# Graph layer on one Trainium2 core: target rows in 16 bits, and the sixteen first feature loads of the node pass issued in steps

## What is computed

```python
row, col = (edge_index[0], edge_index[1])          # src, dst
tp = fctp_messages(node_features[col], edge_attr_tensor, W1, W2, W3, W4)
messages = tp @ Wm + bm
agg = jax.ops.segment_sum(messages, row, num_segments=N_NODES)
upd = jnp.concatenate([node_features, agg], axis=-1) @ Wu + bu
return node_features + upd
...
x = _layernorm(x + ref(x, ...), axis=-1)
```

## Time and profile before

| | |
|---|---|
| median of 3 runs | 1828.5 us (1827.64 to 1835.35) |
| profiled execution, its own time | 1834.27 us |
| its span, first to last instruction | 1832.5 us |
| mean granted TensorE clock | 0.957 of full speed |
| busy: PE, DVE, ACT, POOL | 1581.1, 1594.1, 900.5, 1067.6 us |
| moved by the DMA engines | 490.07 MB, mean 267 GB/s |

### The profile page before, as it was taken

One profiled execution on the slowest core, in us unless ns is written; L12 is line 12 of the kernel. 1 busy time (PEld: TensorE's weight loads), 2 busy tenths in 40 slices (PEclk: granted clock), 3 DMA queues, 4 the chain that ended last, 5 costly groups with the idle time before them and its releaser, 6 DMA issues.

```text
span 1832.5 us, 35242 instructions
## 1 busy us (share of the span) xinstructions
PE 1581.1 (86%) x11572; PEld 876.3 (48%) x11572; DVE 1594.1 (87%) x1825; ACT 900.5 (49%) x1721; POOL 1067.6 (58%) x837
## 2 busy tenths in 40 slices
PE   4167899999999999999999999999999999298882
PEld 2033444545444554545544454445554454276662
DVE  6276699999999999999999999999999996199994
ACT  1123444545444444555544444445554445088885
POOL 3005777777767777776777777767777774211110
PEclk8688999999999999999999999999999999699996
DMA  9996678888888888888888888888888885899994
GB/s 378 404 395 178 157 234 248 245 244 244 256 244 247 246 247 255 256 247 244 249 255 248 243 250 256 248 242 246 246 252 249 255 248 139 287 391 421 416 418 170
DMA packets 174618, 490.07 MB, mean 267 GB/s; under 512 B 48664, under 2 KB 99096, under 8 KB 149484
## 3 DMA queue, kind: packets, MB, share of 16 engines
q1 hardware_dynamic: 91980, 379.42, 57.5%
q0 software_dynamic: 82304, 109.12, 27.2%
q10 hardware_dynamic: 288, 0.95, 0.2%
HBM read 393.10 MB, written 96.31 MB: 267 GB/s over the span
## 4 chain that ended last, share of the span: by engine, by line
DMA 33%; issue 21%; PE 18%; DVE 14%; POOL 9%; ACT 2%; SPq 1%; POOLq 1%; DVEq 0%; ACTq 0%
DMA agg<-summed,row_idx 18%; DVE prod L527 7%; POOL agg L344 6%; DMA agg<-start_rows 5%; DMA prod<-agg 5%; DMA e_sb<-in_e_rep 4%; PE ps L671 4%; PE ps L678 3%; POOL xg L326 3%; PE ps L659 2%; DVE prod L596 2%; DVE prod L515 2%; DVE stats L615 2%; PE ps L733 1%; PE ps L722 1%
## 5 line engine op out<-in xcount | busy, mean ns | idle before, releaser
L344 POOL DMA_INDIRECT agg<-summed,row_idx x392 | 625.4, 1595 | 363.7 <-DMA agg<-summed,row_idx 183.2
L527 DVE TENSOR_TENSOR prod<-ps,e_sb 128x2048 f32<-128x2048 f32 x294 | 655.3, 2285 | 68.3 <-DMA e_sb<-in_e_rep 47.5
L678 PE MATMUL ps<-prod,packed_sb 128*32 128x512 f32 x2744 | 672.4, 607 | 0.8 <-ACT S_sb L398 0.8
L326 POOL DMA_INDIRECT xg<-in_x_rows,dst_sb x392 | 415.7, 1060 | 187.7 <-issue 113.6
L671 PE MATMUL ps<-prod,packed_sb 128*32 128x512 f32 x2352 | 396.3, 603 | 0.0
L535 DVE TENSOR_TENSOR prod<-ps,e_sb 128x3072 f32<-128x3072 f32 x98 | 328.3, 3350 | 0.0
L515 DVE TENSOR_TENSOR prod<-ps,e_sb 128x2048 f32<-128x2048 f32 x98 | 223.8, 2283 | 49.8 <-issue 32.0
L659 PEld LDWEIGHTS ps<-packed_sb,spread 128*128 128x128 f32 x1176 | 127.8, 143 | 221.8 <-issue 104.5
L441 ACT ACTIVATE summed<-ps 128x644 f32<-128x644 f32 x98 | 69.4, 708 | 330.9 <-PE ps L736 234.0
L659 PE MATMUL ps<-packed_sb,spread 128*128 128x128 f32 x1176 | 174.5, 286 | 51.3 <-issue 28.4
L468 ACT ACTIVATE prod<-prod,shift_n,rstd 128x160 f32<-128x160 f32 (+1 forms) x392 | 166.6, 507 | 40.8 <-DVE shift_n L608 40.8
(11 more groups left out here) (62 smaller groups left out, 1702.4 us busy)
## 6 DMA issues: line engine op xcount, KB each, us to landing
e_sb<-in_e_rep SPq DMA_DIRECT2D x98, 1536.0 KB
e_sb<-in_e_rep SPq DMA_DIRECT2D x98, 1024.0 KB
agg<-start_rows SPq DMA_DIRECT2D x49, 640.0 KB, 15.1
prod<-agg SPq DMA_DIRECT2D x48, 640.0 KB, 10.3
out<-prod POOLq DMA_DIRECT2D x48, 640.0 KB, 7.7
row_sb<-in_src_row SPq DMA_DIRECT2D x98, 256.0 KB
prod<-in_x_t SPq DMA_DIRECT2D x25, 640.0 KB, 12.0
e_sb<-in_x_t SPq DMA_DIRECT2D x24, 640.0 KB, 12.7
```

What stands on the lines that cost most here:

```text
L326: nc.gpsimd.indirect_dma_start(xg[g[1] % 2][:, q, :], None, x_rows, bass.IndirectOffsetOnAxis(dst_sb[g[1]][:, q:q + 1].bitcast(U32), 0)).t ...
L344: nc.gpsimd.indirect_dma_start(agg, bass.IndirectOffsetOnAxis(row_idx[g[1]][:, q:q + 1].bitcast(U32), 0), summed[g[1]][:, q // 2, q % 2 * ...
L527: nc.vector.tensor_tensor(prod[g[1] % 2][:, 4 + 4 * i:8 + 4 * i, :].rearrange("p (a b) e -> p a b e", b=2), ps[:, t_bank(g, 1 + i), :].uns ...
L678: return nc.tensor.matmul(ps[32 * quarter:32 * quarter + 32, S_BANK, :], w[:, 32 * half:32 * half + 32], prod[g[1] % 2][:, tile, :], start ...
```

## The change

`row_sb` and its source in memory hold the targets as unsigned 16-bit numbers instead of 32-bit ones; node numbers are below 65,536. ACT reads them in `find_apart` as before.

The sixteen first `xT` loads get other homes, in the order `e_sb[0]`, `e_sb[1]`, `prod[1]`, and other waits. The first four wait until DVE has done the products of group 96, the next four for those of group 97, the last eight for PE's last round. Besides, the loads 0-1, 2-3, 4-5, 6-7, 8-9, 10-12 and 13-15 wait until the first scatters of 190, 191, 192, 193, 194, 195 and 196 pairs have landed.

```diff
-        row_sb = four("row_sb", [P, GE], I32)
+        row_sb = four("row_sb", [P, GE], U16)
...
-        homes = [prod[1][:, :, :], e_sb[0][:, :, :], e_sb[1][:, :, :]]
+        homes = [e_sb[0][:, :, :], e_sb[1][:, :, :], prod[1][:, :, :]]
         xT = [home.rearrange("p n e -> p (n e)")[:, b * NB:(b + 1) * NB]
-              for home, count in zip(homes, (8, 4, 4)) for b in range(count)]
+              for home, count in zip(homes, (4, 4, 8)) for b in range(count)]
...
-            sp.wait_ge(rounds, ROUNDS * n_groups)
             for n in range(AHEAD):
+                if n == 0:
+                    sp.wait_ge(multiplied, USES * (n_groups - 1))
+                if n == 4:
+                    sp.wait_ge(multiplied, USES * n_groups)
+                if n == 8:
+
+                    sp.wait_ge(rounds, ROUNDS * n_groups)
+                if n in (0, 2, 4, 6, 8, 10, 13):
+                    sp.wait_ge(scattered_a, 16 * (2 * n_groups - 6 + min(n // 2, 6)))
                 load_xT(n)
...
+    assert n_nodes < 2 ** 16
...
-        "src_row": src_p.reshape(groups, P, TILES).transpose(0, 2, 1).reshape(groups, 1, GE),
+        "src_row": src_p.reshape(groups, P, TILES).transpose(0, 2, 1).reshape(groups, 1, GE).astype(np.uint16),
```

More of the change, by code:

```diff
@@ L10 @@
 U32 = mybir.dt.uint32
+U16 = mybir.dt.uint16
 ALU = mybir.AluOpType
```

## The result

The changed kernel takes 1805.48 us (median of 5 runs, 1803.95 to 1807.56), the kernel before beside it 1830.45 us (1827.64 to 1835.55). The ratio is 0.9852, 95% interval 0.9825 to 0.9880: 25 us less, inside the range of 1802 to 1827 and beyond the forecast's own span of 1809 to 1822.

What follows compares the result with a forecast made beforehand. DMA was taken to bound the start, VectorE the steady edge pass, both the node pass. Terms -10.2 + 3.5 - 4 - 1.5 = -12.2 us take the profiled 1834.27 to 1822 and the median 1828.5 to 1816 us; range 1802 to 1827.

Steps and rivals of the forecast that it cites:

- Drain, -10.2: Scatter pairs 190 to 195: `xT` loads spread two per pair give periods of 6.5 us, ending 10.2 us earlier.
- the slower rival: Drain: flowing loads slow all six pairs to 10.3 us each, about 1844 us in all; chance 0.05.
- Start of the node pass, +3.5: Loads 13 to 15 queue ahead of the aggregate loads, so the first add comes about 3.5 us later after the last scatter.
- the head start: Node pass start: loads 13 to 15 go 1.8 us before the last pair's second scatter, filling about 1.5 us of empty DMA.
- Steady pass, -4: Steady edge pass: the halved targets' broadcast shortens VectorE's stalls for the vector attributes, about 4 us in all.
- it can bring that load forward by 0 to 0.31 us: Steady edge pass: 131,072 bytes fewer per slot bring the vector attributes' load forward by at most 0.31 us.
- the steady stalls go: Steady edge pass: 0.2 us less a slot removes nearly all VectorE stalls, about 1800 us in all; chance 0.10.
- Start of the edge pass, -1.5: DMA-bound start, to about 126 us: five row loads each save 0.31 us, 1.5 us in all, ends 0 and -3.
- ScalarE, 0: `find_apart` on ACT: four instructions of 500 ns per group take the same time with 16-bit targets.

Runs made afterwards that it cites:

- kernel without steps: The changed kernel without the waits on scatters before the `xT` loads, which go in groups of four, four and eight; 1812.37 us, ratio 0.9881.

## Why the prediction was right, and where it was off

**Drain, -10.2: right.** Measured -9.0 from `moved` of group 97 to the aggregate loads. The mean period was 6.37 us for 6.5. No period came near 8 us, from which the slower rival decides. The last pair took 7.8 us from its start to the aggregate loads where 6.0 was set. The chain of the changed kernel says why:

```profile
1554.42 6.38 DMA agg<-summed,row_idx
...
1560.82 0.33 SPq L291
...
1562.20 7.35 DMA prod<-agg
```

The pair's first scatter landed 6.4 us after its start, with loads 10 to 12 flowing; then SyncE spent 1.4 us on the issue of loads 13 to 15 before it came to the aggregate loads. The last update of the second scatter's semaphore in the trace is at 1561.24. So up to the last landing the drain took 38.7 us from pair 190's start (1522.56), for 38.5 forecast and 48.7 before: -10.0. Another 1.0 us until the aggregate loads is SyncE's issuing.

The slower rival took a pair beside two loads to be as slow as one beside sixteen. It did not come true. Pairs 190 and 191 started 2.8 and 2.5 us after their two loads went out, and most of the loads' data was through before pair 191's packets came, as the two windows above show. Beside pair 189 of the kernel without steps, 1.43 MB of loads moved in 4 us among the packets of one scatter, and the pair took 10.94 us. The Trainium skill has the rule that a DMA engine alternates between its queues (DMA: Bandwidth & Descriptors, "Queues, rings and completion order"). The traces agree with it as the prediction read it, that only the time counts in which loads flow beside the pair. They don't prove it: no run changes the number of loads in flight and leaves the overlap as it is.

**Start of the node pass, +3.5: the sum came out, the head start in it did not.** From the issue of the aggregate loads to the first add it is +3.5 (3.96 to 7.45 us). But the prediction counted from the last landing: there it was 4.0 us before and is 8.4 now (1561.24 to 1569.65), +4.4, above the 7 to 8 us that it named. The term that it had wrong is the head start of 1.8 us: loads 13 to 15 went out only 0.4 us ahead of the last landing, since the two scatters of that pair landed 0.4 us apart (1560.81 and 1561.24). That the +3.5 agrees to the tenth is the choice of the mark. It is not given back: 233.5 and 233.4 us from first add to end. With nothing behind the last pair it went back to 3.97. The Trainium skill's fit of 2.0 us and the bytes at 436 GB/s (same page, "Anatomy of one DMA") is given there for DMAs that GpSimd issues, and these are SyncE's. For the four loads from the first issue on it makes 8.0 us, an estimate. Measured are 8.8 (1560.82 to 1569.65), and the measurement decides.

**Steady pass, -4: mis-sized, and the step that failed is "it can bring that load forward by 0 to 0.31 us".** I priced the halved broadcast by the time it takes of all DMA engines. What stands in the way is the landing of one scatter, and that came 1.0 us sooner in the whole change, 0.7 us with 16 bits alone ("release" 6.12 to 5.14 and 5.38), two to three times the 0.31. From 128 to 256 to 384 KB the first pair's period goes 6.6, 7.2, 7.7 us: 0.5 to 0.6 us for each 128 KB; below 128 KB no run shows a gain in the release. Why the price is about twice the bytes' own time stays open. The objection to the rival "the steady stalls go" was that stalls come singly, up to 1.8 us, and 0.3 us doesn't cover them; 1.0 us covers most. The three waits shown for L527, 21.4 us together, became 2.2 (all its idle time, 25.7 us, became 10.0), so that rival, with a chance of 0.10, is what happened to this term: -17.6 us from the fifteenth group on (303.49 to 297.31 there, 1561.22 to 1537.40 at the end).

**Start of the edge pass, -1.5: not settled.** The fifteenth group begins 6.2 us earlier in the pair of profiles. Over single executions, kernels with 128 KB beside the scatter have it between 297.3 and 301.2 us, those with 256 KB and this order between 301.4 and 303.6. So two single executions differ by 0 to 6 us; the means of six and of three kernels are 298.5 and 302.8, 4.3 us apart. The sign is as forecast, the size above the end of -3 that was given.

**ScalarE, 0: right**, 500 ns for both types.

The number itself, 1816, was 10.5 us too high, chiefly for the one mis-sized term. That the result lies in the range is partly luck: the range reached down to 1802 only to take in half of a rival with a chance of 0.10, and that rival's 1799 to 1800 lies nearer to 1805.5 than the forecast. The profile-to-profile sum of -12.2 stands against -29.4, of which 17.6 + 6.2 = 23.8 in the edge pass against 5.5.

## What to carry to other kernels

A transfer that is "small against the slot" has to be priced by what it does to the transfer beside it that others wait for, here the landing of a scatter that releases the next large load, and not by its share of the engines' bandwidth. Where two chains are nearly even (here VectorE's 14.5 us and two scatter pairs), a fraction of a microsecond on one of them is multiplied by the number of rounds: look for it in single stalls and in who waits for whom. And bulk loads that must run beside a chain of short dependent transfers cost little if they are handed out one portion per link, with the last portion ahead of the last link.

## What was not expected of the hardware

Moving 256 KB as two broadcasts of 128 packets of 1 KB cost 60 us more than one broadcast of 128 packets of 2 KB (1897.22 and 1836.58 us), and the first pair's period went to 8.09 us against 7.23. It is not that there is a second DMA instruction (1812.66 us with the 128 KB in two DMAs), nor a further one of 2 KB (1813.52). Twice as many full packets is what is left, or the doubled reading of one source row; no run parts these.

The broadcast with half of it behind `load_ev` took 1853.26 us, though all of it in the old place takes 1830.93 and all of it behind takes 1816.81. In its stalled slots VectorE got the vector attributes 8.0 us after their issue on average (30 slots), in the kernel before 7.5 (20 slots). Why the half costs more than the whole stays open.
